# A Swin-style block on one core: attention output with fp32 values and weights swapped, moved to channel order by the SP queue

## The reference, cut to what matters

```python
xn  = layernorm(xw)                                  # over the 96 channels of each token
q, k, v = split(xn @ qkv_w.T + qkv_b)                # 12 heads of 8 channels
attn = softmax(einsum('bhnd,bhmd->bhnm', q * SCALE, k) + bias)
out  = einsum('bhnm,bhmd->bhnd', attn, v)            # 49 x 49 times 49 x 8, for each head and window
out  = out.transpose(0, 2, 1, 3).reshape(Bw, N, C) @ proj_w.T + proj_b
seq  = shortcut + out
seq2 = batchnorm(depthwise_conv3x3(seq))
out  = seq2 + gelu(seq2 @ w1.T + b1) @ w2.T + b2     # hidden width 384
```

## Time and profile before

| | |
|---|---|
| median of 3 runs | 4471.49 us |
| the profiled execution: span from the first to the last instruction | 4483.3 us |
| PE busy | 4149.9 us, 93% |
| DVE busy | 4035.2 us, 90% |
| ACT busy | 3540.7 us, 79% |
| POOL busy | 1813.2 us, 40% |
| 16 DMA engines, queue of the kernel's transfers | 25.5% |

### The profile page before, as it was taken

One profiled execution on the slowest core, in us unless ns is written; L12 is line 12 of the kernel. 1 busy time (PEld: TensorE's weight loads), 2 busy tenths in 40 slices (PEclk: granted clock), 3 DMA queues, 4 the chain that ended last, 5 costly groups with the idle time before them and its releaser, 6 DMA issues.

```text
span 4483.3 us, 143736 instructions
## 1 busy us (share of the span) xinstructions
PE 4149.9 (93%) x51980; PEld 2703.3 (60%) x51980; DVE 4035.2 (90%) x7480; ACT 3540.7 (79%) x5891; POOL 1813.2 (40%) x1559
## 2 busy tenths in 40 slices
PE   4999999999999999999999999999999999999998
PEld 2666666666666666666666666666666666666665
DVE  6799999889999999998999899999999998988997
ACT  2688887878878788878888788788788888787886
POOL 3334444444343434434443434344343443434442
PEclk9899999999999999999999999999999999999998
DMA  1222222222222222222222222222222222222221
GB/s 48 69 76 81 77 78 76 78 78 81 77 77 77 77 78 80 76 78 75 80 81 76 79 76 78 76 81 78 76 78 77 80 76 80 75 79 77 80 79 41
DMA packets 363523, 340.69 MB, mean 76 GB/s; under 512 B 67200, under 2 KB 362561, under 8 KB 362708
## 3 DMA queue, kind: packets, MB, share of 16 engines
q1 hardware_dynamic: 362708, 329.89, 25.5%
HBM read 39.48 MB, written 38.54 MB: 17 GB/s over the span
## 4 chain that ended last, share of the span: by engine, by line
DVE 38%; issue 26%; PE 18%; SPq 11%; DMA 4%; ACT 2%; DVEq 1%; ACTq 0%; POOL 0%; POOLq 0%
DVE s L808 11%; DVE mx L777 6%; SPq L278 5%; DVE rec L790 4%; DMA q_bd<-ql 3%; DVE vl L844 3%; DVE on L794 3%; SPq L276 2%; PE a_ps L517 2%; DVE y L838 2%; SPq L319 2%; PE st_ps L368 2%; DVE kl L817 2%; DVE ol L856 2%; PE st_ps L362 2%
## 5 line engine op out<-in xcount | busy, mean ns | idle before, releaser
L680 POOL TENSOR_TENSOR pl<-p,ph 128x588 f16<-128x588 f32 x1024 | 1349.1, 1317 | 1890.5 <-ACT ph L584 1890.5
L808 DVE SCALAR_TENSOR_TENSOR s<-ximg,cols,s 96x392 f32<-96x392 f32 x2048 | 1610.6, 786 | 98.2 <-issue 71.4
L777 DVE TENSOR_REDUCE mx<-sm_ps 128x12 f16<-128x588 f32 x1024 | 780.8, 763 | 126.1 <-PE sm_ps L383 118.5
L581 ACT ACTIVATE p<-st_ps 128x588 f32<-128x588 f32 x1024 | 673.4, 658 | 184.9 <-PE st_ps L368 162.6
L584 ACT ACTIVATE ph<-st_ps 128x588 f16<-128x588 f32 x1024 | 681.9, 666 | 0.0
L517 PE MATMUL a_ps<-g,w_s 128*96 128x392 f32 x1536 | 618.2, 512 | 0.0
L336 PE MATMUL o_ps<-vh,ph 128*128 128x36 f16 x6144 | 559.9, 182 | 1.8 <-POOL pl L680 1.7
L337 PE MATMUL o_ps<-vl,ph 128*128 128x36 f16 x6144 | 551.0, 180 | 0.0
L338 PE MATMUL o_ps<-vh,pl 128*128 128x36 f16 x6144 | 551.0, 180 | 0.0
L336 PEld LDWEIGHTS o_ps<-vh,ph 128*128 128x128 f16 x6144 | 487.3, 96 | 53.2 <-POOL pl L680 2.3
L368 PE MATMUL st_ps<-q_bd,k_st 113*64 113x98 f16 x12288 | 484.3, 214 | 34.0 <-issue 34.0
(11 more groups left out here) (131 smaller groups left out, 8347.0 us busy)
## 6 DMA issues: line engine op xcount, KB each, us to landing
q_st<-qm SPq DMA_DIRECT2D x512, 96.0 KB
q_bd<-qh SPq DMA_DIRECT2D x1024, 48.0 KB
k_st<-kh SPq DMA_DIRECT2D x512, 96.0 KB
x_sb<-in_x SPq DMA_DIRECT2D x256, 147.0 KB, 2.3
out<-y SPq DMA_DIRECT2D x256, 147.0 KB, 2.4
k_bd<-kh SPq DMA_DIRECT2D x512, 48.0 KB
k_st<-kl SPq DMA_DIRECT2D x256, 96.0 KB
q_bd<-ql SPq DMA_DIRECT2D x512, 48.0 KB
```

The lines of the kernel that those rows point to most:

```text
L581: af(p32[:, q % 2, :, :].rearrange("p (b h) n -> p b h n", b=2), src, ACT.Exp)
L680: tt(pl[:, p % 2, :, 0:TOK], p32[:, p % 2, :, :], ph[:, p % 2, :, 0:TOK], ALU.subtract).then_inc(pl_done, 1)
L777: v.tensor_reduce(mx[:, (st[1] - lag) % 2, :, p].rearrange("p (b h) -> p b h", b=2), sm_ps[:, :, 0:HALF].rearrange("p b (h n) -> p b h n", ...
L808: v.scalar_tensor_tensor(acc, image_rows(st, lag, k // 3, k % 3), cw_c[:, k:k + 1], acc, ALU.mult, ALU.add)\
```

## The change

The weights and the moving operand of the product change places, and the product is fp32. v32 (128 x 32 for each head and pair of windows, fp32) is the weight: of its 32 columns, for each of 8 channels, one holds window 0's value, one window 1's, one ones for window 0's rows and one ones for window 1's rows. p32 (49 columns) moves. So the output is in the order channel x token, with the softmax's sums beside it in the same layout, and four heads stand below each other in the four groups of 32 partitions of o_ps. ACT copies o_ps to SBUF (`outputs`, twice a step), and four new SP transfers of 32 rows each sort o_sb into ox: two blocks of outputs and two of sums, 96 channels each. ACT takes ln and exp(-x) of the sums (`inverses`), DVE multiplies once (`normalise`), and the projection is two fp32 matmuls.

Gone are the second exponential, POOL's pl, the tiles vh and vl (DVE's vl step; ACT writes v32 in their place), reciprocals, the four transposes, oh and ol, and 12 fp16 projection matmuls. p32 has four buffers in place of two, and b_proj is added by DVE in the shortcut's instruction.

```diff
@@ sync, step @@
                 if real(st, 8):
                     sp.dma_start(dram_rows(out, out_at), y[0:C, e % 2, :]).then_inc(stored[e % 2], 16)
+                if real(st, 4):
+                    r4 = (e - 4) % 2
+                    wait_for(o_done, c4)
+                    for x4 in range(4):
+                        sp.dma_start(ox[:, r4, x4, :], o_sb[x4::4, r4, :, :]).then_inc(o_in[r4], 16)
                 if real(st, 1):
                     wait_for(kl_done, c1)
                     wait_for(qh_done, c1)
@@ tensor, values_times_p @@
-                    wait(pe, vl_done, st, lag, 2)
-                wait(pe, pl_done, st, lag, NP, q + 1)
+                    wait(pe, v32_done, st, lag, 2)
+                wait(pe, p_done, st, lag, NP, q + 1)
                 if q % 2 == 0:
-                    wait(pe, norm_done, st, lag, 4, q)
-                r, r2 = (st[1] - lag) % 4, q % 2
-                for j in range(NJ):
-                    o = o_ps[:, r2 * 256:r2 * 256 + 2 * HEADS * VW].rearrange("p (w h) -> p w h", w=2)[:, :, j * 2 * VW:(j + 1) * 2 * VW]
...
-                    last = three(o, s_h, s_l, moving(vh), moving(vl))
+                    wait(pe, o_done, st, lag, 2, q // 2)
+                r = (st[1] - lag) % 2
+                for g3 in range(NG):
+                    for c4 in range(4):
+                        h, at = 4 * g3 + c4, (2 * g3 + q % 2) * TOK
+                        last = mm(o_ps[32 * c4:32 * c4 + 32, at:at + TOK], v32[:, r, h, q, :], p32[:, q, h, :], start=True, stop=True)
@@ tensor, projection @@
-                    for h2 in range(2):
...
-                        last = three(o, wp_h[:, 2 * w + h2, :], wp_l[:, 2 * w + h2, :], m_h, m_l,
-                                     start=h2 == 0, stop=h2 == 1)
+                    last = mm(o, wp[:, :], ox[:, (st[1] - 5) % 2, w, :].rearrange("c (n r k) -> c n r k", n=NP, k=WS), start=True, stop=True)
@@ tensor, step @@
                 queries(st)
-                values_times_p(st, 4, 2)
                 max_scores(st, 2, 1)
                 keys(st)
                 second(st, 0)
                 second(st, 1)
+                values_times_p(st, 4, 2)
+                values_times_p(st, 4, 3)
                 max_scores(st, 2, 2)
                 exp_scores(st, 3, 0)
                 values(st)
                 second(st, 2)
                 centred(st)
                 exp_scores(st, 3, 1)
-                values_times_p(st, 4, 3)
                 variance(st)
                 projection(st)
-                channels_first(st)
@@ scalar @@
+            def exp(st, lag, q):
+                wait(act, st_done, st, lag, NP, q + 1)
+                wait(act, pv_done, st, lag + 1, NP, q + 1)
+                af(p32[:, q, :, :]..., st_ps[...], ACT.Exp).then_inc(p_done, 1)
+            def inverses(st):
+                wait_ring(act, o_in, st, 5, 64)
+                wait(act, norm_done, st, 6)
+                af(inv[:, :, :], ox[:, (st[1] - 5) % 2, 2:4, :], ACT.Ln).then_inc(ln_done, 1)
+                wait(act, ln_done, st, 5)
+                af(inv[:, :, :], inv[:, :, :], ACT.Exp, scale=-1.0).then_inc(inv_done, 1)
+            def outputs(st, lag, half):
+                wait(act, pv_done, st, lag, NP, 2 * half + 2)
+                if half == 0:
+                    wait_ring(act, o_in, st, lag + 2, 64)
+                af(o_sb[:, (st[1] - lag) % 2, :, 2 * half * TOK:(2 * half + 2) * TOK], o_ps[...], ACT.Identity).then_inc(o_done, 1)
@@ scalar, step @@
-                exp_both(st, 4, 3, 0)
+                exp(st, 4, 3)
+                inverses(st)
                 high_part(st, b_ps, kh, k_done, kh_done)
-                exp_both(st, 4, 3, 1)
                 masked(st)
                 high_part(st, d_ps, qh, q_done, qh_done)
-                for part in range(2):
-                    exp_both(st, 3, 0, part)
+                outputs(st, 4, 1)
+                exp(st, 3, 0)
...
+                exp(st, 3, 2)
+                outputs(st, 3, 0)
                 gelu(st, 7, 0)
@@ gpsimd: low_part and its four calls a step are gone @@
@@ vector @@
-            def normalise(st, lag, half):
...
+            def normalise(st):
+                r = (st[1] - 5) % 2
+                wait(dve, inv_done, st, 5)
+                v.tensor_tensor(ox[:, r, 0:2, :], ox[:, r, 0:2, :], inv[:, :, :], ALU.mult).then_inc(norm_done, 1)
@@ vector, step @@
                 tap(st, 7, 5)
+                normalise(st)
                 low_part(st, b_ps, kh, kl, kh_done, kl_done)
...
-                if real(st, 2):
-                    for w in range(2):
...
-                        v.scalar_tensor_tensor(lo, b_ps[...], 1 / UP, hi, ALU.mult, ALU.subtract).then_inc(vl_done, 1)
-                normalise(st, 4, 1)
...
-                normalise(st, 3, 0)
```

More of the change, by code:

```diff
@@ L282, in step @@
                 e = st[1]
-                c1, c2, c3, c6, c8 = (count(st, lag) for lag in (1, 2, 3, 6, 8))
+                c1, c2, c3, c4, c6, c8 = (count(st, lag, 1 + (lag == 4)) for lag in (1, 2, 3, 4, 6, 8))
                 x_at, out_at = dram_place(st, -2), dram_place(st, 8)
@@ L457, in values @@
                 last.then_inc(v_done, 1)
[L459 to L470, removed]
             def projection(st):
@@ L571, in _ @@
             act.wait_ge(ready, 4)
-            def exp_both(st, lag, q, part):
+            def exp(st, lag, q):
                 if not real(st, lag):
                     return
-                src = st_ps[:, :, 0:HALF].rearrange("p b (h n) -> p b h n", n=TOK)
-                if part == 0:
-                    wait(act, st_done, st, lag, NP, q + 1)
-                    wait(act, pl_done, st, lag, NP, q - 1)
-                    af(p32[:, q % 2, :, :].rearrange("p (b h) n -> p b h n", b=2), src, ACT.Exp)
-                else:
-                    wait(act, pv_done, st, lag, NP, q - 1)
-                    af(ph[:, q % 2, :, 0:TOK].rearrange("p (b h) n -> p b h n", b=2), src, ACT.Exp).then_inc(ph_done, 1)
+                wait(act, st_done, st, lag, NP, q + 1)
+                wait(act, pv_done, st, lag + 1, NP, q + 1)
+                af(p32[:, q, :, :].rearrange("p (b h) n -> p b h n", b=2),
+                   st_ps[:, :, 0:HALF].rearrange("p b (h n) -> p b h n", n=TOK), ACT.Exp).then_inc(p_done, 1)
+            def inverses(st):
+                if not real(st, 5):
+                    return
+                wait_ring(act, o_in, st, 5, 64)
[4 more added lines that the diff above has]
+            def outputs(st, lag, half):
+                if not real(st, lag):
+                    return
+                wait(act, pv_done, st, lag, NP, 2 * half + 2)
+                if half == 0:
+                    wait_ring(act, o_in, st, lag + 2, 64)
+                af(o_sb[:, (st[1] - lag) % 2, :, 2 * half * TOK:(2 * half + 2) * TOK],
+                   o_ps[:, 0:2 * NG * TOK].rearrange("p (g n) -> p g n", g=NG), ACT.Identity).then_inc(o_done, 1)
             def high_part(st, ps, dst, done, out_):
@@ L652, in step @@
                     af(xh[0:C, st[1] % 2, :, 0:TOK], xn[:, :, :], ACT.Identity).then_inc(xh_done, 1)
-                for part in range(2):
-                    exp_both(st, 3, 2, part)
+                exp(st, 3, 2)
+                outputs(st, 3, 0)
                 gelu(st, 7, 0)
@@ L766, in _ @@
                                   .unsqueeze(2).broadcast_to([TOK, HEADS, NW, TOK]))
+            for r in range(2):
                 for w in range(2):
-                    last = v.memset(vh[64 * w:64 * w + TOK, r, :, w::2, HD:VW], 1.0)
+                    last = v.memset(v32[64 * w:64 * w + TOK, r, :, :, :].rearrange("p h n (d x) -> p (h n d) x", x=4)[:, :, 2 + w], 1.0)
             link(last)
@@ L779, in maxima @@
                  .then_inc(max_done, 1)
-            def normalise(st, lag, half):
-                if not real(st, lag):
+            def normalise(st):
+                if not real(st, 5):
                     return
-                wait(dve, pv_done, st, lag, NP, 2 * half + 2)
-                wait(dve, ot_ps_done, st, lag + 1)
-                o = o_ps[:, :].rearrange("p (n c) -> p n c", n=2)[:, :, 0:2 * HEADS * VW].rearrange("p n (g a d) -> p n g a d", a=2, d=VW)
-                for h2 in range(2):
-                    rows = slice(64 * h2, 64 * h2 + TOK)
-                    v.reciprocal(rec[rows, half, :, :], o[rows, :, :, h2, HD]).then_inc(rec_done, 1)
-                for h2 in range(2):
-                    rows = slice(64 * h2, 64 * h2 + TOK)
-                    wait(dve, rec_done, st, lag, 4, 2 * half + h2 + 1)
-                    v.tensor_tensor(on[rows, 2 * half:2 * half + 2, :].rearrange("p n (g d) -> p n g d", d=HD),
-                                    o[rows, :, :, h2, 0:HD], rec[rows, half, :, :].unsqueeze(3).broadcast_to([TOK, 2, HEADS, HD]),
-                                    ALU.mult).then_inc(norm_done, 1)
+                r = (st[1] - 5) % 2
+                wait(dve, inv_done, st, 5)
```

(1 more changed line is left out.)

128 lines of the change are left out of this document (45 added, 83 removed).

## The result

The changed kernel takes 4966.2 us (median of 4 runs, 4951.11 to 4987.99) against 4471 for the kernel before. The ratio is 1.111 [1.107, 1.114]. The direction was as forecast, but the time is 226 us above the 4740 and 66 us above the range.

The account below looks back on a forecast made before the run. The SP queue's ring was taken to bound the changed kernel: 14.9 + 2.6 = 17.5 us a step, 145 an iteration with 4 + 1 extra, 4640 for 32, plus 105 + 7, 4752; less 12, 4740 us. Range 4500 to 4900.

Parts of the forecast that it names:

- The ring of q_bd<-ql, kh, k_bd, y, q_st and the issues: SP queue's closed loop of issues and waits: 14.9 us a turn before, 17.5 with the four new issues, setting the step.
- The price of an issue: Four new SP transfers, between the store and kl's transfers: 0.65 us each, 2.6 us a step, ends 2.1 and 3.1.
- kh to y: DVE's path from kh done to y done, 3.64 us; q_st follows 3.78 us behind the start of k_bd, unchanged.
- DVE and POOL: DVE loses work, and its taps fall from 786 to near 620 ns as POOL's pl goes; DVE is off the path.
- PE: TensorE's step: 16.4 less 0.5 less 3.8, plus 0.65 projection and 2.1 new product, 14.9 us, below the SP ring.
- Rival 1: PE becomes the bound as small fp32 weight loads don't hide: step 20.0 us, time about 5400 us; chance 0.08.
- Rival 2: SP's four new issues cost 0.2 us together in place of 2.6, so PE's relief shows: 4150 us; chance 0.06.
- Rival 3: The SP ring is shorter, giving back 0.7 to 1.3 us of the added 2.6: 4560 to 4410 us; chance 0.12.
- Rival 4: SP's irregular issues double, 4 us an iteration more: 4870 us, inside the forecast's own range; no chance given.
- 11.12 us from q_st to the next k_bd: Part of the SP ring read from the old trace, taken as unchanged; with 3.78 us it makes the 14.9 us turn.
- PE's time priced at full clock: TensorE's step, with matmuls priced at 2.4 GHz: 14.9 us in a 17.5 us turn, leaving 2.6 us of slack.
- the forecast's extra time outside the turns: Setup and ends at 105 + 7 us, plus 1 us an iteration at the loop's end on top of SP's own.

Follow-up runs that it names:

- the doubled product: The changed kernel with every product of values and probabilities computed twice, the second overwriting the first with the same numbers: 4967.4 us.
- the pad: The changed kernel with one unused tile of 160 bytes a partition ahead of x_sb, restoring tile addresses to multiples of 256 bytes: 4835.2 us.
- Three kernels with a raised clock: Changed kernel with every value product computed twice, 4967.4 us; with 24 idle matmuls, 5063.1 us; with 10 idle matmuls and a 160-byte unused tile, 4808.7 us.

## Why the prediction was right, and where it wasn't

**What bounds the kernel.** Right. The ring of q_bd<-ql, kh, k_bd, y, q_st and the issues sets the turn after the change. The runs without the four transfers, with four in the kernel before, and with eight all move the time by the issues, and the doubled product doesn't.

**The price of an issue.** Taken at 0.65 us, with 2.1 and 3.1 as ends for four. A typical set takes 2.56 us, and the mean is 2.80, because some are stretched. That is 0.20 x 256 = 51 us of the miss. That the four have no cover was right.

**kh to y.** 3.78 forecast, 3.76 measured. The wait for y is there: 189.9 us, 0.74 a turn (0.7 forecast).

**DVE and POOL.** The taps were to fall to about 620 ns without POOL's pl, and fell to 636 from 786. In the kernel before with four more transfers, which keeps pl, they take 709, so removing pl is not the only thing that moves them; no run removes pl alone.

```profile
L744 DVE SCALAR_TENSOR_TENSOR s<-ximg,cols,s 96x392 f32<-96x392 f32 x2048 | 1303.4, 636 | 15.4 <-POOL s L642 2.9
```

**PE.** The product was taken at 2.1 us a step and takes 1.3. That changed nothing: doubling it left the time where it was.

**Rivals.** Rival 1 (PE) fell to the doubled product. Rival 2 (issues nearly free) fell to 0.64 us an issue. Rival 3 (a shorter ring) had the wrong sign. Rival 4 (irregular issues double) didn't come: the other issues were 8.82 us in the mean, where 8.26 + 0.5 was forecast.

**The first failed step: "11.12 us from q_st to the next k_bd", taken over unchanged.** It contains the flight of q_bd<-ql. I treated a duration from the trace before as a property of the transfer, but it belongs to its addresses too, and the removed tiles moved them from a multiple of 256 bytes. The sum had 2.86 us from the end of the q_bd<-ql issue to k_bd; turns at full clock took 3.19, and 2.61 with the pad. It is worth 131 us, shown by the pad: 4966 to 4835, which is inside the range.

**The second failed step: PE's time priced at full clock.** The sum had PE at 14.9 us in a turn of 17.5 and counted the rest as harmless slack. In the changed kernel, where PE waits in most turns, half the clock was granted for 1433 us. In the 20 turns below 0.6 kh never started at the landing but came late by itself. The mean time from the issue to k_bd is 3.59 us, with 3.19 in turns at full clock; 0.40 x 256 gives some 100 us. This is read from the turns of one trace and goes the same way in three others (four more in the kernel before, the aligned one, and that with idle matmuls). Three kernels with a raised clock weren't faster, so its share stays open.

The account: the mean turn is 0.97 us above the forecast's 18.0, in 256 turns 248 us: 187 in the last line of the table, 51 in the ox issues, 15 in the other issues, less 5 ahead of q_st. What stands outside the turns is 51 us less than forecast (93 in place of 144 with the 32 for the loop's ends), and the median lies 17 us above the profiled span where the forecast took off 12, which adds 29: 248 - 51 + 29 = 226. Of the 187, some 100 go with the low-clock turns and the rest with the longer flight. The pad gave back more than this rest, 131 us (108 by the mean turn, 18.97 to 18.55), because at the old remainder the last line would have been 2.61 at full clock and not the 2.86 of the sum. That the forecast's extra time outside the turns covered 51 us of the miss is luck.

## What to carry to other kernels

Before adding transfers to a queue that lies in a ring, follow the ring around and ask which wait the queue has anyway; the same four transfers cost 808 us behind the wait for y, about 330 in the wait for kh and 220 on POOL's queue, each measured against the kernel without them. A change that removes tiles moves all addresses behind them, so check the new addresses before you take over durations of transfers: here a remainder of 96 by 256 in place of 0 cost 131 us. Slack on TensorE that comes as a wait in most turns went with a lower clock here: price the turns at the lower clock as well, at least as the upper end of the range.

## What the runs showed of the hardware that I had not expected

- The same SBUF-to-SBUF transfer lands 0.6 to 0.7 us later (2.70 for 2.01 us in the median) when its tiles begin 96 bytes past a multiple of 256.
- Fp32 matmuls of 49 columns into four column groups start 7, 7 and 6 ns apart and the next four 24 ns later: 44 ns for four. With the change-over ahead and behind, 48 take 0.66 us at full clock.
- Four transfers from POOL's queue take POOL 2.27 us to issue, 0.57 each, and the landing of q_bd<-ql from SP's queue beside them came 3.12 us after its issue in place of 2.71 (medians).
- Half the granted clock for 29% of the span, with TensorE busy 86% of it by the profile: a high busy share doesn't say that the clock is granted.
